# The wait between the two squares of a gated cross-attention and spiking-FFN kernel

## The reference

```python
# 1: gated mLSTM attention: q = layernorm(x), k = v = ctx, 8 heads of 32
ig, fg = gates of (q, k, v); cs = cumsum(log_sigmoid(fg))
log_D = tril(cs[s] - cs[t]) + ig[t]
C = (q k^T / sqrt(32)) * exp(log_D - rowmax)
h = C / (max(|sum C|, exp(-rowmax)) + 1e-6) @ v
x = x + tanh(g_xattn) * layernorm(h) * ln_scale

# 2: gated spiking feed-forward, hidden width 1024
h = square(relu(layernorm(x) @ W_fc.T))
y = h @ W_proj.T
# five steps: reset = mem > 1; mem = 0.9 mem + y - reset; spike = mem > 1
x = x + tanh(g_ffn) * (number of spikes) / 5
```

## Time and profile before

| | us |
|---|---|
| median of 3 runs | 659.78 (659.73 to 660.92) |
| the profiled execution | 662.98 |
| its span, first to last instruction | 661.2 |
| PE busy in the span | 589.5 (89%) |
| DVE busy | 542.4 (82%) |
| ACT busy | 484.4 (73%) |
| POOL busy | 485.6 (73%) |
| granted clock of PE, mean | 0.972 |

### The profile page before, as it was taken

How to read it: one execution, slowest core, us unless ns; L and a number is a source line. 1 busy time by engine, 2 the same in 40 slices (tenths; PEclk the granted TensorE clock), 3 DMA queues, 4 the chain that set the end, 5 groups by cost and what they waited for, 6 DMA issues and landing times.

```text
span 661.2 us, 17665 instructions
## 1 busy us (share of the span) xinstructions
PE 589.5 (89%) x6032; PEld 483.9 (73%) x6032; DVE 542.4 (82%) x1222; ACT 484.4 (73%) x1011; POOL 485.6 (73%) x531
## 2 busy tenths in 40 slices
PE   1265887799999999999999999999999999999795
PEld 0155776778787878787788878787878777787684
DVE  4878787889989998899989998999888998958522
ACT  4555777678787888788878878788878867676463
POOL 6157678867996969787897799787969788675232
PEclk9996799999999999999999999999999999999898
DMA  8915553845276335916573538642680556300000
GB/s 262 225 52 115 97 115 70 176 83 96 83 156 169 74 91 147 208 26 139 115 186 60 96 110 155 159 86 80 150 207 18 97 101 148 63 2 33 1 33 32
DMA packets 73192, 71.33 MB, mean 108 GB/s; under 512 B 8720, under 2 KB 68752, under 8 KB 73104
## 3 DMA queue, kind: packets, MB, share of 16 engines
q1 hardware_dynamic: 71888, 70.00, 47.3%
q10 hardware_dynamic: 1216, 0.21, 0.2%
HBM read 27.44 MB, written 8.39 MB: 54 GB/s over the span
## 4 chain that ended last, share of the span: by engine, by line
PE 51%; DVE 10%; issue 10%; ACT 7%; POOL 7%; SPq 4%; DMA 2%; POOLq 0%; ACTq 0%; DVEq 0%
PE z_ps L997 16%; PE y_ps L1057 16%; PE arg_ps L702 3%; PE qk_ps L717 3%; POOL sq_lo L1040 3%; DVE spikes L1075 3%; PE misc_ps L463 2%; SPq L650 2%; PE misc_ps L529 2%; SPq L513 2%; ACT sq_hi L1019 1%; POOL c_lo L746 1%; PE pv_ps L766 1%; PE pv_ps L764 1%; PE pv_ps L841 1%
## 5 line engine op out<-in xcount | busy, mean ns | idle before, releaser
L1040 POOL TENSOR_TENSOR sq_lo<-w_raw,sq_hi 128x512 fp32r<-128x512 f32 (+1 forms) x96 | 113.0, 1178 | 66.2 <-ACT w_raw L1020 66.1
L746 POOL TENSOR_TENSOR c_lo<-decay 128x512 bf16<-128x512 f32 x128 | 132.5, 1042 | 22.4 <-DVE decay L736 22.2
L997 PE MATMUL z_ps<-x_hi,wfc_hi 128*128 128x512 f32 (+1 forms) x288 | 115.7, 402 | 5.9 <-ACT w_raw L1007 4.1
L1057 PE MATMUL y_ps<-sq_hi,wpr_hi 128*128 128x512 f32 (+1 forms) x288 | 115.1, 400 | 1.1 <-POOL sq_lo L1040 1.1
L997 PE MATMUL z_ps<-x_hi,wfc_lo 128*128 128x512 f32 (+1 forms) x288 | 107.2, 372 | 0.0
L997 PE MATMUL z_ps<-x_lo,wfc_hi 128*128 128x512 f32 (+1 forms) x288 | 107.2, 372 | 0.0
L1057 PE MATMUL y_ps<-sq_lo,wpr_hi 128*128 128x512 f32 (+1 forms) x288 | 106.8, 371 | 0.0
L1057 PE MATMUL y_ps<-sq_hi,wpr_lo 128*128 128x512 f32 (+1 forms) x288 | 106.6, 370 | 0.0
L736 DVE TENSOR_TENSOR decay<-qk_ps,decay 128x512 f32<-128x512 f32 x128 | 87.1, 680 | 18.5 <-PE qk_ps L717 14.4
L728 ACT ACTIVATE decay<-arg_ps,lqk_col 128x512 f32<-128x512 f32 x128 | 86.5, 676 | 19.7 <-PE arg_ps L705 19.1
L1040 POOL TENSOR_TENSOR sq_lo<-relu,sq_hi 128x512 fp32r<-128x512 f32 (+1 forms) x48 | 56.3, 1173 | 37.9 <-ACT relu L1020 35.2
(11 more groups left out here) (139 smaller groups left out, 1686.2 us busy)
## 6 DMA issues: line engine op xcount, KB each, us to landing
x_in<-x SPq DMA_DIRECT2D x32, 256.0 KB, 3.5
kT_in<-ctx_cols SPq DMA_DIRECT2D x32, 256.0 KB, 3.8
v_in<-ctx_rows SPq DMA_DIRECT2D x32, 256.0 KB, 3.2
k_stack<-kT_hi SPq DMA_DIRECT2D x64, 128.0 KB, 3.4
k_stack<-kT_lo SPq DMA_DIRECT2D x64, 128.0 KB, 3.7
q_stack<-qT_hi SPq DMA_DIRECT2D x64, 128.0 KB, 4.0
q_stack<-qT_lo SPq DMA_DIRECT2D x64, 128.0 KB, 4.2
out<-w_raw SPq DMA_DIRECT2D x32, 256.0 KB, 3.6
```

The source lines that it names most:

```text
L746: e.tensor_tensor(c_lo[i % NCH][:, :], c, top(c), ALU.subtract).then_inc(sem("c_lo"), 1)
L997: ins = e.matmul(z_ps[:, tokens(q)], lhsT, rhs, start=(n == 0), stop=(n == len(terms) - 1))
L1040: e.tensor_tensor(sq_lo[n % NSQ][:, tokens(q)], relu[n % NRE][:, tokens(q)], sq_hi[n % NSQ][:, tokens(q)].bitcast(fp32), ALU.subtract).the ...
L1057: ins = e.matmul(y[:, c, :], w[:, j, c * P:(c + 1) * P], h, start=(j == 0 and i == 0 and (c == 0 or whole)), stop=(j == FT - 1 and i == 2) ...
```

## The change

In `square` the first activation no longer goes through `link`. It has no increment, and no wait stands between it and the in-place square that follows it. Both read the same relu tile, and the second also writes it; that the second writes behind the reads of the first is left to the engine, which runs the two in order. All the other waits and increments stay.

```diff
--- before.py
+++ after.py
@@ -1016,7 +1016,7 @@
             if n - NSQ >= 0:
                 e.wait_ge(sem("y"), n - NSQ + 1)
             r = relu[n % NRE][:, tokens(q)]
-            link(e, "scalar", e.activation(sq_hi[n % NSQ][:, tokens(q)], r, ACT.Square))
+            e.activation(sq_hi[n % NSQ][:, tokens(q)], r, ACT.Square)
             e.activation(r, r, ACT.Square).then_inc(sem("square"), 1)
 
         def job_cols(tile, q):
```

## The result

The changed kernel is slower. Its median is 664.27 us (20 runs, 662.42 to 666.33) against 660.83 us for the kernel before on the same chip (20 runs, 658.43 to 663.89): a ratio of 1.0046, with a 95% interval of 1.0032 to 1.0060. Forecast was 657.4 us, with a range from 655.8 to 659.5.

The account below looks back on a forecast made before the run. The loop was taken as bound by PE's own work, so only shortened PE waits count. Ramp 0.24, loop 1.5, late part 0.12 and tail 0.52 sum to 2.4 us: 659.78 to 657.4 us, range 655.8 to 659.5.

Parts of the forecast that it names:

- The saving per square: On ACT, the 0.04 gap before each in-place square becomes a 0.09 overlap: 0.12 us each, 17.3 us for 144.
- The rival that the second square waits for the drain of the first: On ACT, the in-place square starts only after the one before has drained, so nothing shortens: 659.8 us, chance 0.06.
- The period, first effect: In each loop period, earlier sq_lo brings L615, x_lo and the first z 0.08 us earlier; 0.5 us over six.
- The period, second effect: In the loop, the chain to s_lo comes earlier, so PE's waits at L841 go: 0.9 us plus 0.1.
- The loop's sum: Both effects over six loop periods: 1.5 us saved, bounds 0 and 2.2.
- The ramp: Before the loop, two squares on the chain, at 82.25 and 83.28, save 0.24 us.
- Late part and tail: After the loop: 0.12 us at PE's 541.19 wait; in the tail 0.16, 0.24 and 0.12, together 0.52.
- Slower: the hold: Earlier GpSimd starts hold a small DVE operation 0.94 us longer, once per loop period: 663.0, half hidden 660.5; chance 0.07.

Follow-up runs that it names:

- ramp only: Kernel before, with the wait removed only from the squares of steps 6 and 7 of the first job; 662.88 us, ratio 1.0026.
- the gate step first: GpSimd's sq_lo of step 6 of even jobs waits for L612, L615, L616: on the change 659.04 us (0.9961), on the kernel before 660.62 us (1.0004).
- the change once more: The changed kernel run again unaltered, against the kernel before on another chip; 664.87 us, ratio 1.0069.

## Why the prediction was wrong

**The sum first.** From 657.4 to 664.27 it is 6.9 us. Of this 1.05 is the starting point (659.78 from three runs, 660.83 from twenty), 2.4 the gain that did not come, and 3.4 the loss that came in its place.

**The saving per square: right.** 0.14 us from start to start in the median of all squares, 0.13 in the period followed, 0.12 taken, and the half-width squares lose the same, as was said. ACT's busy time fell by 16.3 us; the 17.3 forecast count the gap of 0.04 as well, which was never busy time. The rival that the second square waits for the drain of the first is out. The Trainium skill's rule that was weighed there (VectorE: DVE Perf Modes, section "The DRAIN you can't avoid": a semaphore between chained operations costs nothing) does not carry over to ACT.

**The period, first effect: this is a step that failed.** It said that with L1020 earlier, `sq_lo`, L615, `x_lo` and z come earlier alike. `sq_lo` did come earlier against DVE's list, by 0.15. But L612, which was not among the rows, started 0.07 ahead of `sq_lo`, and this distance was shorter than the move. They changed places, and the first z came 0.14 later in place of 0.08 earlier. `sq_lo` was to get longer against DVE; it got shorter, 1.30 after 1.52, since L612 now waits for it.

**The period, second effect: the step that cost most.** The chain to `s_lo` was said to pass "the small ACT and DVE steps", all of which follow. `off` is a DVE step beside this chain, and it does not follow GpSimd's start: it was held 0.8 us longer, and `x1ln`, the squares and the `sq_lo` behind it came late with it. The waits at L841 went from 0.9 us (five) to 1.8 (six). Their size was no safe ground either: "ramp only", with the same loop as before, has one such wait of 0.2 us. That the chain to `s_lo` gets shorter where no new hold meets it was right: with the gate step first, these waits are 1.7 us (six) with the square waits and 0.3 (one) without.

**The loop's sum** was -1.5 for six periods and came out at +3.1 for five, by the profiles. The three losses of a period, 0.54, make 2.7 of it. One wait of 0.82 at L529 (228.57) comes on top, less what some longer pauses of PE gave back. That wait too has a hold behind it: `qT_lo`, for which PE waits, comes after an `off` that `sq_lo` held.

```profile
226.51 1.20 DVE L374 SCALAR_TENSOR_TENSOR off<-mv,rstd 128x2 f32<-128x2 f32 x1
227.63 0.68 DVE L492 TENSOR_TENSOR qT_lo<-misc_ps,qT_hi 128x512 bf16<-128x512 f32 x1
```

**The ramp**: -0.24 forecast, +1.2 found. The hold of 3.42 us was nowhere in the forecast: between the fourth and fifth `row_max` the seven profiles with this hold take 68.2 us on average (67.0 to 69.2), the seven without 67.1 (66.0 to 67.9). Clock and hold are mixed in this. Where the clock is 1.00 the stretch takes 67.6 with the hold (two profiles) and 66.8 without (four); where it is 0.91, 68.2 (three) and 67.5 (three). So the hold is worth roughly 0.7 to 0.9 us, and the lower clock some 0.5 to 0.7 more; within a group the profiles spread by 0.8 to 1.6. Two squares alone bring the hold.

**Late part and tail: right in the rows.** The waits at 541.19 and 617.70 of the earlier trace rows are gone: PE's shift against before falls there by 0.15 and 0.16. The z at 634.92 comes 0.27 earlier against the list ahead of it (0.24 forecast), the last y 0.15 (0.12). In the one profile of after, a different phase of the clock near 630 hides it. The average over all profiles agrees, though the two ranges overlap: the seven with the waits in the tail have 141.6 us on average (140.0 to 142.2), the seven without 140.8 (139.5 to 142.0).

**The rivals.** "Slower: the hold" was the mechanism, with a chance of 0.07. Its price of 0.94 for one operation in each period was about right as size but wrong in place: L612's hold mostly replaces L615's, and `off` brings most of the loss against before. That its 663.0 lies near the measured time is therefore in part luck. Against it stood that both engines' starts "hang on the same step and move together". That was the error: DVE's L612 follows DVE's own list, only GpSimd's start hangs on the square. The distance, 0.07 us, could have been read in the trace before, and so could the fact that `off` was already held once in each period.

**What stays open.** Why a held `off` is passed over for a second GpSimd instruction. At the place of `am_part`, it was held once (1.02 to 1.03) where DVE had been idle for 0.15 us or more before it, once or twice (1.10 to 1.11, or 2.02 to 2.03) where the idle time was 0.01 to 0.05, and always over both where it came directly behind L736. The distances do not separate the middle cases. Nor is it enough elsewhere to come directly behind another operation: the `off` at 226.51 above came directly behind L361, and was held over `sq_lo` alone, though the next GpSimd instruction followed that without a pause. In the ramp, six of the seven held `off` start 0.01 to 0.05 behind the start of `kw`, and the three short ones 0.11 to 0.13 ahead of it; but in "the change once more" `off` starts 0.43 ahead of it and is held over five instructions all the same. Open too is where the 0.3 to 0.4% sits that the change is worth behind the gate step: the medians show it, the five periods of the profiles do not (356.0 against 356.1, 354.2 against 353.8), and the tail is only some 0.8 us of it. That this is about the 2.4 us of the forecast (0.36%) does not confirm the forecast's terms. In the pair with the gate step first, the 1.4 us that PE no longer waits at L841 stand against a pause at L808 that grew from 1.0 to 2.2.

## What to carry to other kernels

Before a wait is removed, list for every instruction released earlier what DVE starts within the move on either side; here a DVE operation with two SBUF inputs that GpSimd overtook was charged a whole GpSimd instruction or more (L612 1.08 us more, `off` 0.8 in the loop and 3.2 in the ramp), and the tiny one, with the layer norm behind it, cost most. Where order decides and not work, an added wait that fixes the better order can be faster than none: with the gate step first the ratio went from 1.0046 to 0.9961. Where the order can't be fixed, the form can: `off` by columns, one tensor and a scalar each, was not held anywhere.

## What the runs showed of the hardware

- Two activations of 128x512 that read the same tile, the second in place, start 0.52 us apart with no wait and 0.66 with one (medians of 112). The Trainium skill, ScalarE: Activation LUTs, section "What ACT_TABLE_LOAD costs", has back-to-back activations overlap by about 93 ns; the 0.09 here agrees.
- DVE operations alone, and held while a GpSimd instruction that started first is in work: 32x256 with two SBUF inputs 0.41 and 1.49 us; 32x128 with one tensor and a scalar read from SBUF 0.27 and 1.21; 128x2 with two inputs 0.13, up to 1.25 over one instruction and 1.82 to 2.03 over two; 128x4 with two inputs 0.15, and 3.33 to 3.47 over five GpSimd instructions in a row.
- 128x1 with one tensor and a scalar read from SBUF is not held: 0.18 to 0.22 us each in all 128 cases of each of four kernels, 76 of which started while GpSimd was at work; 0.33 for two in a row. L615 has the same form and is held, so the width counts or the mode that comes with it; the runs do not tell which.
- In the ramp the granted clock was at the lower level for about 3 us in some profiles (0.91 over 20 us), for about 7 us in two (0.83) and not at all in others (1.00), and two profiles of the same kernel differed in it (0.91 and 1.00). A 256-column matmul then takes 415 ns in place of some 280.
